# A fused feed-forward and window-attention kernel: the later chunks are normalised on GpSimd and not on ScalarE

## The chip, the cores and the metric

The kernel runs on one core of a Trainium2 chip. The metric is the device time of one execution in microseconds (us), as a median of three runs. The engines are TensorE (PE in the profile), VectorE (DVE), ScalarE (ACT), GpSimd (POOL) and SyncE (SP), which here issues most of the DMAs.

## The reference, cut to what matters

The input x is 4 batches of 2048 tokens with 256 numbers each, in float32. It goes through an expert layer, an attention layer and the same expert layer again, each of them on a layer norm of x and added to x:

```python
x = x + 0.5 * ffn(layernorm(x))      # 8 experts, top 2, an expert over its capacity is dropped
x = x + attn(layernorm(x))           # 16 heads of 16, |distance| <= 128, token 0 global
x = x + 0.5 * ffn(layernorm(x))

def layernorm(x, eps=1e-05):
    m = mean(x, axis=-1); v = var(x, axis=-1)
    return (x - m) / sqrt(v + eps)
```

With the inputs of this case every expert is over its capacity, so that the expert layers add nothing; the kernel counts this on the chip and then skips them. What is left is the attention over 4 x 2048 tokens and the counting. The layer norm ahead of the attention is what the change touches.

## The kernel before, in words

**Tiling.** A batch is 2048 tokens: 16 tiles of 128 tokens on the 128 partitions, or 4 chunks of 4 tiles. The 16 heads go in 4 groups of 4 heads. The main loop has 4 batches x 4 groups x 16 tiles = 256 steps of 4 quarters, one for each head of the group. In a quarter TensorE makes the scores of a query strip for the row maximum ("A", L1065), VectorE adds the mask and takes the maximum (L1514), TensorE makes the transposed scores of a tile 20 steps further back ("B", L1099), ScalarE takes their exponential (L1243), and TensorE multiplies probabilities with values ("PV", L1117), 23 steps back. At the end of each step GpSimd clears the two corners outside of the window in the exponentials of that B ("CUT", L1313 and L1318), once the fourth exponential is there; PV waits for it (`band_ready`).

**The layer norm of a chunk.** The input of the next batch is made ready while the loop runs on the batch before. SP loads a chunk into `x_ring`; VectorE takes the moments of its four tiles (L707, L709, "MOMENTS"); GpSimd makes `rstd`, `std_first` and `shift` of them (L720 to L734, "RSTD", the power at L728 first); then four instructions "NORM" write the tiles of `xn` (ScalarE at L1156, `scale * x + bias`), TensorE transposes them in two halves of two tiles ("XT", L890, p = 0 and p = 1) into two shared PSUM banks, and ScalarE copies each half out into `xnT` (L1175). The projections QK (L954) read that. ScalarE cuts their result into three bfloat16 pieces with VectorE and GpSimd (PIECE1 L1193, REST L1442, PIECE2 L1208, PIECE3 L1301), which SP stacks by DMA. In the first batch VectorE does the four NORMs of each chunk itself; so there are 3 x 4 = 12 chunks with 48 NORMs on ScalarE. They are the "later chunks" here.

**What sets the order.** Every engine walks the same list of events and runs its own in that order. The list is made by tables of quarters. Relative to the quarter at which a chunk begins, RSTD stands at 7, the NORMs at 12, 14, 16 and 18 and XT at 19. CUT stands at the end of a step. An engine runs in order, so that a waiting instruction holds all that is behind it on its engine.

The waits around the change: ScalarE's first NORM waits for `shift_ready` and for the transposes of the chunk before, of its second half (`xn` is one buffer). XT waits for `xn_ready`, 2 tiles for p = 0 and 4 for p = 1, and for its PSUM bank. The functions that the diff touches:

Of the kernel before, what the change touches and what calls it, by code (L numbers as in the profile page):

```python
# [7 lines left out]
ALU = mybir.AluOpType  # L8
# [41 lines left out]
def build(nc, x, wqk, wback, wv, wo, gate, w1, b1, w2, b2, consts, x1, out):  # L50
    ctx = ExitStack()
    with ctx:
        def sb(name, shape, dt=FP32):
# [10 lines left out]
        xn = sb("xn", [P, 4, D])  # L64
# [29 lines left out]
        mean_var = sb("mean_var", [P, 2, 4, 2])  # L94
# [41 lines left out]
                 "wqk_ready", "pads_ready", "k_ones", "v_pads", "wback_in",  # L136
                 "stats_ready", "moments_ready", "eps_added", "rstd_ready", "shift_ready", "xn_ready",
                 "base_ready", "logits_in", "move_ready", "moved", "fold_ready",
# [12 lines left out]
        S = sems  # L151
# [435 lines left out]
        def attend(nb, dram, batch_at, tiles_at, first):  # L587
# [123 lines left out]
            def deviations(pool, i):  # L711
# [6 lines left out]
                if i >= 2 and order[i - 2][0] == "EARLY":  # L718
                    pool.wait_ge(*normed(i - 2))
                pool.tensor_scalar(var_eps[:, :], mean_var[:, i % 2, :, 1], EPS, None, ALU.add)\  # L720
# [77 lines left out]
            def run_sync(sp):  # L798
# [17 lines left out]
                    for kind, *n in events:  # L816
                        if kind == "LOAD":
                            i, = n
                            if i in slot_of:
                                m, lap = slot_of[i]  # L820
                                if lap:
                                    before = ring[ring.index(i) - 3]
                                    if before in store_of:
                                        sp.wait_ge(S["moments_ready"], 4 * (before + 1))
                                        sp.wait_ge(*store_of[before])
                                    else:
                                        sp.wait_ge(*normed(before))
# [43 lines left out]
            def run_tensor(pe):  # L871
# [272 lines left out]
            def run_scalar(act):  # L1144
# [4 lines left out]
                    for kind, *n in events:  # L1149
                        if kind == "NORM" and not on_vector(n[0]):  # L1150
                            i, t = n
                            if t == 0:
                                act.wait_ge(S["shift_ready"], i + 1)
                                if early_count[i]:
                                    act.wait_ge(*filled("XT", early[early_count[i] - 1], 1))
                            act.activation(xn[:, t, :], x_tiles(i)[:, t, :], ACT.Identity,  # L1156
                                           bias=shift[:, i % 2, t:t + 1], scale=rstd[:, i % 2, t:t + 1])\
                               .then_inc(S["xn_ready"], 1)
                        elif kind == "FOLD_IN":
# [100 lines left out]
            def run_gpsimd(pool):  # L1260
                    for kind, *n in events:
                        if kind == "RSTD":
                            deviations(pool, *n)
                        elif kind == "FILL":
                            pool.memset(v_heads[:, :, 0:H, HD], 1.0).then_inc(S["v_pads"], 1)
# [73 lines left out]
            def run_vector(dve):  # L1339
# [12 lines left out]
                    for kind, *n in events:  # L1352
                        if kind == "MOMENTS":
                            moments(dve, *n)
                        elif kind == "NORM" and on_vector(n[0]):
                            i, t = n
                            if t == 0:
                                dve.wait_ge(S["rstd_ready"], i + 1)
                                if early_count[i]:
                                    dve.wait_ge(*filled("XT", early[early_count[i] - 1], 1))  # L1360
                            dve.tensor_scalar(xn[:, t, :], x_tiles(i)[:, t, :], mean_var[:, i % 2, t, 0:1],
                                              rstd[:, i % 2, t:t + 1], ALU.subtract, ALU.mult)\
                               .then_inc(S["xn_ready"], 1)
                        elif kind == "ROUTE":
# [186 lines left out]
                        elif kind == "OUT_MULT":  # L1551
                            n, = n
                            g, quartet = divmod(n, 4)
                            if g == 0:
                                dve.wait_ge(*normed(early_index[0, quartet]))
                            elif g % NG == 0:
                                dve.wait_ge(*filled("TURN_ATTN", late_index[g // NG - 1, quartet], 1))
# [131 lines left out]
```

## Time and profile before

| | us |
|---|---|
| median of 3 runs (852.82 to 858.6) | 853.02 |
| the profiled execution | 855.22 |
| its span in the profile | 853.5 |
| PE busy | 812.3 (95%) |
| DVE busy | 743.6 (87%) |
| ACT busy | 633.6 (74%) |
| POOL busy | 480.4 (56%) |
| the 48 NORMs on ACT (L1156) | 29.0 |

An engine's busy time is the union of its instructions' spans. "Idle before" is the time for which the engine stood still ahead of an instruction, with who ended it. The granted TensorE clock is at its full level in all 40 slices of the profile.

### The profile page before, as it was taken

Reading aid. Unit: us, or ns where it says so; the run is one execution under the profiler, and the core shown is the slowest. Engines: PE = TensorE matmul, PEld = TensorE weight load, DVE = VectorE, ACT = ScalarE, POOL = GpSimd, SP = SyncE. Lnnn points to the kernel's source line nnn. Section 1 sums busy time; section 2 is a strip of 40 time slices with the busy share of each in tenths; the row PEclk is TensorE's granted clock in tenths of the full one; section 3 lists DMA queues with packets and bytes.
Section 4 is the critical chain, followed back from the end, with each engine's and each line's share of the span. In section 5 each row is a group of like instructions: output and inputs, shape, how many; then the busy total and the mean of one; then the engine's idle time right before and its main releaser. Section 6 shows DMA issues by size and latency. Waiting matters only on the chain.

```text
span 853.5 us, 50532 instructions
## 1 busy us (share of the span) xinstructions
PE 812.3 (95%) x21504; PEld 613.5 (72%) x21505; DVE 743.6 (87%) x2788; ACT 633.6 (74%) x1418; POOL 480.4 (56%) x856
## 2 busy tenths in 40 slices
PE   9798999999999999999999999999999999998897
PEld 8555667677788777667778777766777877766675
DVE  7798799998987899998988889998988789999864
ACT  2258978997877666898777766799777766788871
POOL 3212556775554475766554556767555546656772
PEclk9999999999999999999999999999999999999999
DMA  7632224342213335342222235533221233423003
GB/s 227 107 94 64 67 77 125 102 130 61 82 57 103 104 107 164 113 124 82 71 77 65 91 114 149 166 102 92 68 80 57 94 113 101 141 76 128 7 27 106
DMA packets 93210, 83.55 MB, mean 98 GB/s; under 512 B 17584, under 2 KB 92208, under 8 KB 92976
## 3 DMA queue, kind: packets, MB, share of 16 engines
q1 hardware_dynamic: 91376, 78.91, 30.6%
q8 instruction: 172, 2.82, 1.5%
q10 hardware_dynamic: 1600, 1.31, 1.0%
q14 instruction: 62, 0.51, 0.2%
HBM read 20.66 MB, written 8.39 MB: 34 GB/s over the span
## 4 chain that ended last, share of the span: by engine, by line
PE 71%; DVE 13%; ACT 9%; issue 4%; POOL 1%; DMA 1%; SPq 1%; ACTq 0%; DVEq 0%; POOLq 0%
PE bank L1117 14%; PE bank L1065 12%; PE bank L1099 12%; PE bank L954 11%; PE bank L969 7%; DVE bank L1514 6%; PE bank L937 6%; ACT probs L1243 4%; PE bank L1139 3%; PE bank L923 2%; PE bank L875 2%; PE bank L890 1%; DVE row_max L1514 1%; ACT pieces L1193 1%; ACT xn L1156 1%
## 5 line engine op out<-in xcount | busy, mean ns | idle before, releaser
L1243 ACT ACTIVATE probs<-bank 128x384 f32<-128x384 f32 (+1 forms) x1024 | 459.5, 481 | 141.5 <-PE bank L1099 125.2
L1514 DVE CUSTOM_DVE_ANT_0 bank<-bank,con 128x288 f32<-128x288 f32 x1024 | 494.5, 519 | 55.7 <-PE bank L1065 47.5
L1065 PE MATMUL bank<-k_stack,q_stack 96*32 96x288 bf16 x4096 | 326.8, 288 | 8.7 <-DVE row_max L1514 4.8
L1099 PE MATMUL bank<-q_stack,k_stack 99*32 99x288 bf16 (+3 forms) x4096 | 320.1, 284 | 11.4 <-ACT probs L1243 7.7
L1117 PE MATMUL bank<-probs,v_sb 128*32 128x128 f32 x5888 | 307.1, 272 | 5.9 <-issue 4.2
L1313 POOL TENSOR_SCALAR_AFFINE_SELECT probs<-probs 128x512 f32<-128x512 f32 x240 | 154.7, 645 | 176.2 <-ACT probs L1243 175.6
L1117 PEld LDWEIGHTS bank<-probs,v_sb 128*32 128x32 f32 x5888 | 194.6, 110 | 38.8 <-issue 8.0
L1065 PEld LDWEIGHTS bank<-k_stack,q_stack 96*32 96x32 bf16 x4096 | 128.2, 95 | 69.6 <-DVE row_max L1514 19.9
L1099 PEld LDWEIGHTS bank<-q_stack,k_stack 99*32 99x32 bf16 x4096 | 125.5, 95 | 68.3 <-ACT probs L1243 43.8
L1318 POOL TENSOR_SCALAR_AFFINE_SELECT probs<-probs 128x512 f32<-128x512 f32 x240 | 153.0, 637 | 18.2 <-ACT probs L1243 18.2
L954 PE MATMUL bank<-xnT,wqk_sb 128*32 128x256 f32 x2048 | 159.7, 381 | 0.6 <-DVE neg_max L1536 0.5
L1514 DVE DVE_READ_ACCUMULATOR2_ANT row_max<- 128x1 f32 x1024 | 144.2, 141 | 0.0
L1301 POOL TENSOR_TENSOR pieces<-rest,pieces 128x512 bf16<-128x512 f32 x64 | 74.5, 1163 | 62.7 <-ACT pieces L1208 62.4
L969 PE MATMUL bank<-wv_sb,xnT 128*32 128x272 f32 x1024 | 84.3, 393 | 1.7 <-ACT v_sb L1215 1.1
L937 PE MATMUL bank<-wo_sb,attnT 128*32 128x264 f32 x1024 | 72.2, 386 | 0.4 <-DVE x_ring L1422 0.2
L954 PEld LDWEIGHTS bank<-xnT,wqk_sb 128*32 128x32 f32 x2048 | 65.0, 111 | 6.0 <-ACT v_sb L1215 1.2
L1193 ACT ACTIVATE pieces<-bank 128x512 bf16<-128x512 f32 x64 | 38.3, 598 | 21.5 <-PE bank L954 20.8
L1442 DVE TENSOR_TENSOR rest<-bank,pieces 128x512 f32<-128x512 f32 x64 | 44.1, 689 | 6.3 <-ACT pieces L1193 6.1
L1208 ACT ACTIVATE pieces<-rest 128x512 bf16<-128x512 f32 x64 | 40.6, 635 | 7.5 <-DVE rest L1442 7.4
L1139 PE MATMUL bank<-con,o_raw 128*32 128x68 f32 x2048 | 44.0, 223 | 1.9 <-ACT o_raw L1256 1.5
L1330 POOL TENSOR_TENSOR glob_term<-v_all,p 128x272 f32<-128x272 f32 x64 | 41.4, 647 | 2.2 <-DVE v_all L1483 1.8
L707 DVE BATCH_NORM_STATS2 stats<-x_ring 128x6 f32<-128x256 f32 x100 | 42.1, 421 | 0.0
(123 smaller groups left out, 714.4 us busy)
## 6 DMA issues: line engine op xcount, KB each, us to landing
q_stack<-pieces SPq DMA_DIRECT2D x384, 64.0 KB, 2.7
k_stack<-pieces SPq DMA_DIRECT2D x364, 64.0 KB, 2.7
x_ring<-in_x SPq DMA_DIRECT2D x28, 512.0 KB, 4.7
out_x<-x_ring SPq DMA_DIRECT2D x15, 512.0 KB, 4.3
attn<-in_x SPq DMA_DIRECT2D x4, 512.0 KB, 6.3
wback_sb<-in_wback SPq DMA_DIRECT2D x8, 256.0 KB, 5.6
k_stack<-pieces ACTq DMA_DIRECT2D x20, 64.0 KB, 3.6
q_stack<-neg_max SPq DMA_DIRECT2D x48, 16.0 KB, 2.2
```

What stands on the lines that cost most here:

```text
L937: last = pe.matmul(bank_of("PROJECT", i, t)[SP * s:SP * (s + 1), 0:D + E], attnT[:, t // 2, k, at:at + SP], wo_sb[:, k, :], start=(k == 0) ...
L954: last = pe.matmul(bank_of("QK", g, c)[SP * s:SP * (s + 1), 256 * half:256 * (half + 1)], wqk_sb[:, g % NG, k, SP * s:SP * (s + 1)], xnT[: ...
L969: last = pe.matmul(bank_of("VALUES", b, t)[SP * s:SP * (s + 1), 0:D + HD], xnT[:, k, at:at + SP], wv_sb[:, k, :], start=(k == 0), stop=(k ...
L1065: last = pe.matmul(a_ring[i % len(a_ring)][SP * s:SP * (s + 1), 0:WIN], q_stack[g % 2][0:KROWS, h, q:q + SP], k_stack[g % 2][0:KROWS, h, q ...
L1099: last = pe.matmul(score_bank(i)[SP * s:SP * (s + 1), start:final], k_stack[g % 2][0:SROWS, h, WINDOW + P * j + SP * s:WINDOW + P * j + SP ...
L1117: last = pe.matmul(o_bank[SP * h:SP * (h + 1), P * (i % 4):P * (i % 4 + 1)], v_sb[:, j, VW * head:VW * head + SP], probs[:, j % 4, h, P * ...
L1139: last = pe.matmul(bank_of("TURN", n)[SP * s:SP * (s + 1), HG * VW * i:HG * VW * (i + 1)], o_raw[:, at:at + SP], take, start=True, stop=True)
L1243: act.activation(probs[:, j % 4, h, c0:c1], score_bank(i)[:, c0:c1], ACT.Exp, scale=LOGIT_SCALE).then_inc(S["exp_ready"], 1)
L1301: pool.tensor_tensor(pieces[i % PIECES][:, 2, :], rest[:, :], pieces[i % PIECES][:, 1, :], ALU.subtract).then_inc(S["piece3_ready"], 1)
L1313: pool.affine_select(out=part, in_=part, compare_op=ALU.is_ge, fill=0.0, base=0, pattern=[[0, HG], [1, P]], channel_multiplier=-1).then_in ...
L1318: pool.affine_select(out=part, in_=part, compare_op=ALU.is_ge, fill=0.0, base=0, pattern=[[0, HG], [-1, P]], channel_multiplier=1).then_in ...
L1514: dve.tensor_tensor_reduce(out=a_ring[i % len(a_ring)][:, 0:WIN], in0=a_ring[i % len(a_ring)][:, 0:WIN], in1=mask, scale=1.0, scalar=con[: ...
```

## The change

All four NORMs of each later chunk move from ScalarE to GpSimd, at the same places of the list of events. They are written there as VectorE does them in the first batch, `(x - mean) * rstd` with two per-partition operands, and not as `scale * x + bias`; so they wait for `rstd_ready` and not for `shift_ready`. The semaphore `xn_ready` becomes two, `normed0` and `normed1`, one for each half of a chunk: XT of half p waits for its own, and the first NORM of each half waits for the transposes of the same half of the chunk before. The other users of `xn_ready` wait for both.

```diff
+        NORM_ENGINES = ("gpsimd", "gpsimd")
...
-            def normed(i):
-
-                return S["xn_ready"], 4 * early_count[i + 1]
-
-            def on_vector(i):
-
-                return first and order[i][1] == 0
+            def normed(i, half):
+
+                return S[f"normed{half}"], 2 * early_count[i + 1]
+
+            def norm_engine(i, t):
+
+                return "vector" if first and order[i][1] == 0 else NORM_ENGINES[t // 2]
...
-                            pe.wait_ge(S["xn_ready"], 4 * early_count[i] + 2 * p + 2)
+                            pe.wait_ge(*normed(i, p))
...
-                        if kind == "NORM" and not on_vector(n[0]):
+                        if kind == "NORM" and norm_engine(*n) == "scalar":
                             i, t = n
-                            if t == 0:
+                            if t % 2 == 0:
                                 act.wait_ge(S["shift_ready"], i + 1)
                                 if early_count[i]:
-                                    act.wait_ge(*filled("XT", early[early_count[i] - 1], 1))
+                                    act.wait_ge(*filled("XT", early[early_count[i] - 1], t // 2))
...
+                        elif kind == "NORM" and norm_engine(*n) == "gpsimd":
+                            i, t = n
+                            if t % 2 == 0:
+                                pool.wait_ge(S["rstd_ready"], i + 1)
+                                if early_count[i]:
+                                    pool.wait_ge(*filled("XT", early[early_count[i] - 1], t // 2))
+                            pool.tensor_scalar(xn[:, t, :], x_tiles(i)[:, t, :], mean_var[:, i % 2, t, 0:1],
+                                               rstd[:, i % 2, t:t + 1], ALU.subtract, ALU.mult)\
+                                .then_inc(S[f"normed{t // 2}"], 1)
```

GpSimd's queue is where the order matters. The line numbers differ by a few in the changed kernel: L720 to L734 of before are L722 to L736, L1301 is L1313, L1313 and L1318 are L1325 and L1330, and the new NORM is L1273. This is GpSimd in the third chunk (c = 2) of the second batch, before, from RSTD on:

```order
L728 TENSOR_TENSOR rstd<-var_eps,neg_half 128x4
L732 TENSOR_TENSOR std_first<-var_eps,rstd 128x4
L734 TENSOR_TENSOR shift<-neg_mean,rstd 128x4
L1313 AFFINE_SELECT probs<-probs 128x4x128
L1318 AFFINE_SELECT probs<-probs 128x4x128
L1313 AFFINE_SELECT probs<-probs 128x4x128
L1318 AFFINE_SELECT probs<-probs 128x4x128
L1301 TENSOR_TENSOR pieces<-rest,pieces 128x512
L1313 AFFINE_SELECT probs<-probs 128x4x128
L1318 AFFINE_SELECT probs<-probs 128x4x128
```

and the same place with the change:

```order
L730 TENSOR_TENSOR rstd<-var_eps,neg_half 128x4
L734 TENSOR_TENSOR std_first<-var_eps,rstd 128x4
L736 TENSOR_TENSOR shift<-neg_mean,rstd 128x4
L1325 AFFINE_SELECT probs<-probs 128x4x128
L1330 AFFINE_SELECT probs<-probs 128x4x128
L1273 TENSOR_SCALAR xn<-x_ring,mean_var,rstd 128x256
L1325 AFFINE_SELECT probs<-probs 128x4x128
L1330 AFFINE_SELECT probs<-probs 128x4x128
L1273 TENSOR_SCALAR xn<-x_ring,mean_var,rstd 128x256
L1313 TENSOR_TENSOR pieces<-rest,pieces 128x512
L1273 TENSOR_SCALAR xn<-x_ring,mean_var,rstd 128x256
L1325 AFFINE_SELECT probs<-probs 128x4x128
```

The fourth NORM follows behind the L1330 that comes next. So the one for which XT of p = 1 waits stands behind three CUTs and PIECE3. In the second chunk (c = 1) the queue is RSTD, two CUTs, two NORMs, PIECE3, L1325, two NORMs, L1330; in the fourth (c = 3) it is RSTD, CUT, NORM, PIECE3, NORM, CUT, two NORMs, CUT (its first eight entries behind RSTD, two NORMs in one row):

```order
L1325 AFFINE_SELECT probs<-probs 128x4x128
L1330 AFFINE_SELECT probs<-probs 128x4x128
L1273 TENSOR_SCALAR xn<-x_ring,mean_var,rstd 128x256
L1313 TENSOR_TENSOR pieces<-rest,pieces 128x512
L1273 TENSOR_SCALAR xn<-x_ring,mean_var,rstd 128x256
L1325 AFFINE_SELECT probs<-probs 128x4x128
L1330 AFFINE_SELECT probs<-probs 128x4x128
L1273 TENSOR_SCALAR xn<-x_ring,mean_var,rstd 128x256 x2
```

On ScalarE the four L1156 are gone, and the exponentials (L1243) between which they stood follow each other. The order of TensorE and VectorE is the same row by row.

## Rows read from the trace of the kernel before

**Rows 1.** The page: busy time of the engines, and the chain that ended last

```profile
PE 812.3 (95%) x21504; PEld 613.5 (72%) x21505; DVE 743.6 (87%) x2788; ACT 633.6 (74%) x1418; POOL 480.4 (56%) x856
...
PE 71%; DVE 13%; ACT 9%; issue 4%; POOL 1%; DMA 1%; SPq 1%; ACTq 0%; DVEq 0%; POOLq 0%
```

**Rows 2.** Stretches of time, second batch (last row: fourth), busy time of each engine

```profile
core 0: us, PE busy (x) PEld busy (x) DVE busy (x) ACT busy (x) POOL busy (x), PEclk, DMA share, GB/s
152.80:157.80 5.00, 4.89 (x117) 3.78 (x105) 4.51 (x20) 4.64 (x14) 3.63 (x8) 1.00 0.23 70
164.60:169.30 4.70, 4.36 (x117) 2.51 (x106) 4.63 (x19) 4.62 (x12) 3.90 (x7) 1.00 0.27 88
175.20:180.50 5.30, 4.33 (x133) 2.92 (x125) 4.54 (x17) 5.30 (x14) 4.23 (x8) 1.00 0.61 119
180.50:188.30 7.80, 7.80 (x228) 6.29 (x228) 7.36 (x31) 6.93 (x17) 5.34 (x11) 1.00 0.27 88
188.40:193.20 4.80, 4.01 (x169) 3.14 (x157) 4.76 (x22) 4.80 (x13) 3.55 (x5) 1.00 0.23 73
...
576.60:581.90 5.30, 4.28 (x133) 2.64 (x125) 4.54 (x17) 5.30 (x14) 4.23 (x7) 1.00 0.73 132
```

**Rows 3.** Groups by line: out<-in, shapes, count | busy us, mean ns | idle before

```profile
L1330 POOL TENSOR_TENSOR glob_term<-v_all,p 128x272 f32<-128x272 f32 x64 | 41.4, 647 | 2.2 <-DVE v_all L1483 1.8 <-DVE bank L1543 0.4
...
L725 POOL TENSOR_SCALAR neg_mean<-mean_var 128x4 f32<-128x4 f32 x16 | 3.6, 226 | 1.3
...
L1306 POOL MEMSET wback_sb<- 128x256 f32 x4 | 1.2, 312 | 1.7 <-PE bank L998 1.7
...
L1156 ACT ACTIVATE xn<-x_ring,shift,rstd 128x256 f32<-128x256 f32 x48 | 29.0, 604 | 0.6 <-POOL shift L734 0.6
```

**Rows 4.** Timeline of GpSimd, second chunk (c = 1): start, us, instruction, idle before

```profile
166.35 0.63 POOL L1318 TENSOR_SCALAR_AFFINE_SELECT probs<-probs 128x512 f32<-128x512 f32 x1
167.79 1.16 POOL L1301 TENSOR_TENSOR pieces<-rest,pieces 128x512 bf16<-128x512 f32 x1 [0.80 <-ACT pieces L1208]
168.90 0.65 POOL L1313 TENSOR_SCALAR_AFFINE_SELECT probs<-probs 128x512 f32<-128x512 f32 x1
170.12 0.63 POOL L1318 TENSOR_SCALAR_AFFINE_SELECT probs<-probs 128x512 f32<-128x512 f32 x1 [0.56 <-ACT probs L1243]
```

**Rows 5.** Timeline of GpSimd, third chunk (c = 2)

```profile
175.17 0.64 POOL L1313 TENSOR_SCALAR_AFFINE_SELECT probs<-probs 128x512 f32<-128x512 f32 x1
175.76 0.63 POOL L1318 TENSOR_SCALAR_AFFINE_SELECT probs<-probs 128x512 f32<-128x512 f32 x1
176.35 0.63 POOL L1313 TENSOR_SCALAR_AFFINE_SELECT probs<-probs 128x512 f32<-128x512 f32 x1
...
178.57 1.16 POOL L1301 TENSOR_TENSOR pieces<-rest,pieces 128x512 bf16<-128x512 f32 x1 [1.00 <-ACT pieces L1208]
```

**Rows 6.** Timeline of GpSimd, fourth chunk (c = 3)

```profile
188.91 0.63 POOL L1318 TENSOR_SCALAR_AFFINE_SELECT probs<-probs 128x512 f32<-128x512 f32 x1
...
191.81 0.63 POOL L1318 TENSOR_SCALAR_AFFINE_SELECT probs<-probs 128x512 f32<-128x512 f32 x1
193.71 0.63 POOL L1313 TENSOR_SCALAR_AFFINE_SELECT probs<-probs 128x512 f32<-128x512 f32 x1 [1.26 <-ACT probs L1243]
```

**Rows 7.** Timeline of GpSimd, first chunk (c = 0)

```profile
156.06 0.34 POOL L1290 TENSOR_TENSOR p_arg<-s0T,row_max 128x60 f32<-128x60 f32 x1 [1.28 <-DVE row_max L1501]
...
157.09 0.63 POOL L1318 TENSOR_SCALAR_AFFINE_SELECT probs<-probs 128x512 f32<-128x512 f32 x1
```

**Rows 8.** Timeline of TensorE at XT of the first and fourth chunk

```profile
157.79 0.66 PE L890 MATMUL bank<-con,xn 128*128 128x128 f32 x4
158.93 0.30 PE L890 MATMUL bank<-con,xn 128*128 128x128 f32 x1 [0.48 <-DVE neg_max L1536]
...
193.15 1.09 PE L890 MATMUL bank<-con,xn 128*128 128x128 f32 x8
```

**Rows 9.** The same of the second and third chunk, windows that end inside XT

```profile
169.29 0.98 PE L890 MATMUL bank<-con,xn 128*128 128x128 f32 x7
...
180.49 0.76 PE L890 MATMUL bank<-con,xn 128*128 128x128 f32 x5
```

More of the change, by code:

```diff
@@ L136, in build @@
                  "wqk_ready", "pads_ready", "k_ones", "v_pads", "wback_in",
-                 "stats_ready", "moments_ready", "eps_added", "rstd_ready", "shift_ready", "xn_ready",
+                 "stats_ready", "moments_ready", "eps_added", "rstd_ready", "shift_ready", "xn_ready", "normed0", "normed1",
                  "base_ready", "logits_in", "move_ready", "moved", "fold_ready",
@@ L718, in deviations @@
                 if i >= 2 and order[i - 2][0] == "EARLY":
-                    pool.wait_ge(*normed(i - 2))
+                    for half in range(2):
+                        pool.wait_ge(*normed(i - 2, half))
                 pool.tensor_scalar(var_eps[:, :], mean_var[:, i % 2, :, 1], EPS, None, ALU.add)\
@@ L826, in run_sync @@
                                     else:
-                                        sp.wait_ge(*normed(before))
+                                        for half in range(2):
+                                            sp.wait_ge(*normed(before, half))
                                 sp.dma_start(x_tiles(i), rows(dram, i)).then_inc(S[f"x_ring{m}"], 16)
@@ L1149, in run_scalar @@
                     for kind, *n in events:
-                        if kind == "NORM" and not on_vector(n[0]):
+                        if kind == "NORM" and norm_engine(*n) == "scalar":
                             i, t = n
-                            if t == 0:
+                            if t % 2 == 0:
                                 act.wait_ge(S["shift_ready"], i + 1)
                                 if early_count[i]:
-                                    act.wait_ge(*filled("XT", early[early_count[i] - 1], 1))
+                                    act.wait_ge(*filled("XT", early[early_count[i] - 1], t // 2))
                             act.activation(xn[:, t, :], x_tiles(i)[:, t, :], ACT.Identity,
                                            bias=shift[:, i % 2, t:t + 1], scale=rstd[:, i % 2, t:t + 1])\
-                               .then_inc(S["xn_ready"], 1)
+                               .then_inc(S[f"normed{t // 2}"], 1)
                         elif kind == "FOLD_IN":
@@ L1263, in run_gpsimd @@
                             deviations(pool, *n)
+                        elif kind == "NORM" and norm_engine(*n) == "gpsimd":
[6 more added lines that the diff above has]
+                                               rstd[:, i % 2, t:t + 1], ALU.subtract, ALU.mult)\
+                                .then_inc(S[f"normed{t // 2}"], 1)
                         elif kind == "FILL":
@@ L1354, in run_vector @@
                             moments(dve, *n)
-                        elif kind == "NORM" and on_vector(n[0]):
+                        elif kind == "NORM" and norm_engine(*n) == "vector":
                             i, t = n
-                            if t == 0:
+                            if t % 2 == 0:
                                 dve.wait_ge(S["rstd_ready"], i + 1)
                                 if early_count[i]:
-                                    dve.wait_ge(*filled("XT", early[early_count[i] - 1], 1))
+                                    dve.wait_ge(*filled("XT", early[early_count[i] - 1], t // 2))
                             dve.tensor_scalar(xn[:, t, :], x_tiles(i)[:, t, :], mean_var[:, i % 2, t, 0:1],
                                               rstd[:, i % 2, t:t + 1], ALU.subtract, ALU.mult)\
-                               .then_inc(S["xn_ready"], 1)
+                               .then_inc(S[f"normed{t // 2}"], 1)
                         elif kind == "ROUTE":
@@ L1554, in run_vector @@
                             if g == 0:
-                                dve.wait_ge(*normed(early_index[0, quartet]))
+                                for half in range(2):
+                                    dve.wait_ge(*normed(early_index[0, quartet], half))
                             elif g % NG == 0:
```

## The prediction

> **What bounds the kernel now.** The page comes first. TensorE is busy for 95% of the span and holds 71% of the chain that ended last, VectorE 13% and ScalarE 9%; GpSimd is busy for 56% and holds 1% of it [rows 1]. By these averages ScalarE's work is mostly hidden and GpSimd has room. But the change touches only twelve short places, so the stretches decide. I cut the second batch at the four places where ScalarE normalises a chunk, from its first NORM to XT [rows 2]. In the third chunk (175.2 to 180.5) ScalarE is busy for all of 5.30 us and TensorE for 4.33; in the fourth 4.80 of 4.80 against 4.01; in the second 4.62 of 4.70 against 4.36, with VectorE at 4.63; in the first 4.64 of 5.00 against 4.89. The reader is to see two things. These are the places where ScalarE holds TensorE back, by 0.11, 0.34, 0.97 and 0.79 us: 2.2 us in a batch, 6.6 us in three. And between them, as from 180.5 to 188.3, TensorE is busy throughout, so that what XT loses or gains goes straight into the time. The last row of the group is the same chunk two batches later: 4.28 of 5.30 against 4.33 of 5.30. The batches repeat, and I work out one and multiply by three.
>
> The timelines of GpSimd come next [rows 4 to 7], because GpSimd's spare time is not spread evenly either: in the third chunk it is busy for 4.23 of 5.30 us ahead of XT [rows 2], and its queue there begins late, with the moments and RSTD. Last the start of XT on TensorE [rows 8, 9], which is what the new NORMs must be in time for.
>
> **What is removed.** 48 NORMs of 0.604 us on ScalarE, 29.0 us busy [rows 3]. Behind them stand the exponentials that free TensorE's score banks, so TensorE can reach XT earlier, at most by the idle time above: 6.6 us in all. ScalarE's 0.6 us of waiting for `shift` goes too; it lies within those stretches.
>
> **What is added: the price of a NORM on GpSimd.** No row has it: 128x256, one tensor in, two operations, two per-partition operands. The nearest rows: TENSOR_SCALAR over 4 elements takes 0.226 us (L725) [rows 3]; the one-input select over 512 takes 0.63 to 0.65 and the next one starts 0.59 after it [rows 4, 5]. A straight line between them gives 0.226 + 0.41 x 252/508 = 0.43 for 256 elements. I take 0.45 with a start-to-start distance of 0.40, since two per-partition operands are more than one constant. Below, the bound is a fill of 128x256, 0.31 (distance 0.26); above, a two-input operation over 272, 0.65 (distance 0.60) [rows 3]; the far bound is the two-input subtraction over 512, 1.16 (distance 1.11) [rows 4].
>
> The Trainium skill, GPSIMD Engine Reference, section "Engine selection", speaks against the change: elementwise work belongs to VectorE, as a two-input operation is about twice as slow on GpSimd, while a one-input one runs at about line rate. Its section "Elementwise — side-by-side cycle accounting" gives about 2.6 cycles an element for two inputs at 1.2 GHz. An estimate from that page for 256 elements is 555 ns if the per-partition operands counted like a second input, and the sum below would then be about +6 us in place of +2.6; with its 1.03 cycles for a short body it is 220 ns and a fixed part.
>
> **Where the NORMs land.** Each of the four chunks is followed through GpSimd's new queue, from a CUT that stands ahead of the NORMs and so stays where it is. A CUT costs 2 x 0.59, PIECE3 1.11 to the next start [rows 4].
>
> - Second chunk. The last CUT starts at 166.35, so GpSimd is free at 166.94. Two NORMs to 167.74; this lies in the 0.80 us for which it waited for PIECE2 anyway, and PIECE3 stays at 167.79. The next select starts at 168.90 and is done with its place at 169.49 [rows 4]. The last two NORMs end at 169.49 + 0.80 + 0.05 = 170.34. XT began at 169.29 [rows 9]; its eight transposes took 1.09 in all in the fourth chunk [rows 8], so p = 1 began near 169.84. Now it begins near 170.40: **+0.56**.
> - Third chunk. GpSimd is free at 176.35 [rows 5]. NORM to 176.75, CUT to 177.93, NORM to 178.33, PIECE3 to 179.44 (it waited for ScalarE until 178.57, with ScalarE's PIECE2 now earlier), NORM to 179.84, CUT to 181.02, NORM done at 181.47. XT of p = 1 began near 180.49 + 0.55 = 181.04 [rows 9], now near 181.52: **+0.5**.
> - Fourth chunk. Free at 188.91 + 0.59 = 189.50 [rows 6]. NORM, PIECE3, NORM to 191.41, CUT to 192.59, two NORMs done at 193.44. p = 1 began near 193.15 + 0.55 = 193.70 [rows 8], now near 193.50, if TensorE comes 0.2 earlier, and its 0.79 us of idle time allow for that: **-0.2**.
> - First chunk. The first two NORMs fall into the 1.28 us ahead of L1290 [rows 7]. The other two start at 157.09 + 0.59 = 157.68 and end at 158.53. p = 1 waits for its PSUM bank from VectorE (L1536) and begins at 158.93 [rows 8]: **0**. VectorE is the cover here; without it this chunk would gain at most its 0.11.
>
> Sum: 0.86 us a batch, **+2.6 us** in three. The point is that the 6.6 us TensorE could gain do not come through: it reaches XT earlier in the second and third chunk and then waits there for the last NORM. What is late next is `normed1`.
>
> **What costs nothing.** The selects behind the NORMs start up to 0.8 us later. In the fourth chunk the next one waited 1.26 us for exponentials [rows 6], so it has room; the L1318 behind the second chunk's NORMs goes from 170.12 to about 170.3 [rows 4]. The RSTDs and the CUTs right behind them stand ahead of the NORMs. SP's load of the next chunk waits for `normed` some half a microsecond longer and is issued far ahead of its use; no DMA is added. The finer semaphores take one wait away that had long been met. If this cover were gone, PV would wait for CUT, by the same 0.4 to 0.8 us a chunk, up to 7 us.
>
> The profiled execution took 855.22 us and its span is 853.5; the median is 853.02. The sum on the profiled execution gives 857.8. The prediction is for the median: 853.0 + 2.6 = **855.6 us**.
>
> **The rivals.**
>
> A. *The relief wins.* A NORM costs 0.31 like the fill. Then the second chunk comes to +0.27, the third to -0.1, the fourth to -0.76: -0.6 a batch, -1.8 in all, **851.2**. The limit, if GpSimd were never late, is 853.0 - 6.6 = 846.4. For it: the select's slope is that of a streaming operation. Against it: VectorE is busy for 4.76 of 4.80 in the fourth chunk [rows 2], so that TensorE can hardly come 0.76 earlier, and two operations are not a fill. Chance 0.22.
>
> B. *GpSimd becomes the bound: slower.* Place: `normed1`, for which XT of p = 1 waits. Price: 0.65 a NORM (distance 0.60). The second chunk becomes 166.94 + 1.20, PIECE3 to 169.25, select to 169.84, NORMs done at 171.09: +1.3. The third gains four times 0.20 on its 0.47: +1.3, the fourth +0.6, the first +0.05. That is 3.25 a batch, +9.8, **862.8**. By the same steps the sum turns from gain to loss at a NORM of 0.36, and passes 8.5 us at one of 0.62; that is the point from which this rival decides. For it: the operation has three things to read. [...] Chance 0.2.
>
> C. *The software path is slow*, 1.16 like the subtraction of L1301. Then +3.35, +3.3, +2.6 and +1.05 in the four chunks, 10.3 a batch, +31, **884**. Against it: that row has twice the elements and two inputs. Chance 0.05.
>
> That the NORMs do not move at all is excluded: the new order has them in GpSimd's queue.
>
> The forecast has 0.53. About 1% (8.5 us) is what a measurement of this kernel can tell from no change. Faster by more than that, under 844.5, lies below even the limit: 0.02. Slower by more, over 861.5, is the upper half of B and all of C: 0.17. Within: 0.81. The range goes from 850, which holds most of A, to 863, the end of B.
>
> **What would show it.** L1273 on GpSimd, 48 times, 0.40 to 0.50 us. No L1156. TensorE waits at XT (L893) for `xn` from GpSimd in the second and third chunk, 0.5 us and more each, where before it had exponentials to wait for. ScalarE's busy time falls by 29 us to about 605, GpSimd's grows by some 21 to about 502. PE's idle time moves from the exponentials to XT. Wrong would be: a NORM above 0.62 or below 0.35; PV waiting for CUT in more places than before; or VectorE's instructions getting longer while GpSimd normalises.

## The result, and the profile after

The changed kernel takes **913.6 us** (median of 4 runs, 912.2 to 915.9) against 852.9: a ratio of 1.0709, 95% interval 1.0675 to 1.0743. It is 61 us slower, where +2.6 was forecast and 863 was the end of the range. The profiled execution took 913.2 us, its span is 911.5.

The page of the changed kernel, busy time and the chain that ended last, and of section 2 the granted clock in 40 slices:

```profile
PE 836.1 (92%) x21504; PEld 623.3 (68%) x21505; DVE 747.1 (82%) x2788; ACT 620.4 (68%) x1370; POOL 537.8 (59%) x904
...
PEclk9999999789999999888999999997899999999999
...
PE 60%; POOL 14%; DVE 11%; issue 6%; ACT 4%; SPq 2%; DMA 2%; ACTq 0%; POOLq 0%; DVEq 0%
```

GpSimd went from 1% of the chain [rows 1] to 14%, while its busy share hardly moved, from 56% to 59%. The clock line, all nines before, has three dips, at the three groups of later chunks. The group of the new NORM, and the waits of TensorE at XT (who waited for whom: us in total, times, the longest):

```profile
L1273 POOL TENSOR_SCALAR xn<-x_ring,mean_var,rstd 128x256 f32<-128x256 f32 x48 | 58.5, 1223 | 0.0
```

```profile
PEld bank L893 <- POOL xn L1273: 45.0, 18, 4.3
PE bank L893 <- POOL xn L1273: 40.7, 14, 4.1
```

A NORM takes 1.223 us, twice the 0.604 of ScalarE [rows 3] and 2.7 times the 0.45 that the sum took. All 48 lie between 1.215 and 1.241, which speaks against contention, as that would make some longer than others. GpSimd's queue in the third chunk of the second batch, which answers to [rows 5]:

```profile
182.00 0.64 POOL L1325 TENSOR_SCALAR_AFFINE_SELECT probs<-probs 128x512 f32<-128x512 f32 x1
182.60 0.63 POOL L1330 TENSOR_SCALAR_AFFINE_SELECT probs<-probs 128x512 f32<-128x512 f32 x1
183.23 1.23 POOL L1273 TENSOR_SCALAR xn<-x_ring,mean_var,rstd 128x256 f32<-128x256 f32 x1
184.42 0.63 POOL L1325 TENSOR_SCALAR_AFFINE_SELECT probs<-probs 128x512 f32<-128x512 f32 x1
185.01 0.63 POOL L1330 TENSOR_SCALAR_AFFINE_SELECT probs<-probs 128x512 f32<-128x512 f32 x1
185.63 1.22 POOL L1273 TENSOR_SCALAR xn<-x_ring,mean_var,rstd 128x256 f32<-128x256 f32 x1
186.82 1.16 POOL L1313 TENSOR_TENSOR pieces<-rest,pieces 128x512 bf16<-128x512 f32 x1
187.96 1.23 POOL L1273 TENSOR_SCALAR xn<-x_ring,mean_var,rstd 128x256 f32<-128x256 f32 x1
189.14 0.65 POOL L1325 TENSOR_SCALAR_AFFINE_SELECT probs<-probs 128x512 f32<-128x512 f32 x1
189.74 0.64 POOL L1330 TENSOR_SCALAR_AFFINE_SELECT probs<-probs 128x512 f32<-128x512 f32 x1
190.36 1.23 POOL L1273 TENSOR_SCALAR xn<-x_ring,mean_var,rstd 128x256 f32<-128x256 f32 x1
```

GpSimd has no gap from 182.00 to 191.59. TensorE at the same place:

```profile
186.91 0.66 PE L893 MATMUL bank<-con,xn 128*128 128x128 f32 x4 [0.17 <-POOL xn L1273]
191.64 1.11 PE L893 MATMUL bank<-con,xn 128*128 128x128 f32 x4 [4.08 <-POOL xn L1273]
192.68 0.43 PE L1068 MATMUL bank<-k_stack,q_stack 96*32 96x288 bf16 x4
192.90 0.45 PE L1102 MATMUL bank<-q_stack,k_stack 99*32 99x288 bf16 x4
193.14 0.46 PE L1068 MATMUL bank<-k_stack,q_stack 96*32 96x288 bf16 x4
```

The second half of XT starts 0.05 us after the fourth NORM. And what follows is slower: four matmuls of L1068 or of L1102 took 0.30 us ahead of XT and take 0.43 to 0.46 behind it. Stretches of time around this wait; PEclk, the granted clock, is the third number from the end:

```profile
core 0: us, PE busy (x) PEld busy (x) DVE busy (x) ACT busy (x) POOL busy (x), PEclk, DMA share, GB/s
182.00:187.00 5.00, 4.69 (x149) 3.16 (x142) 4.78 (x18) 4.91 (x12) 5.00 (x8) 1.00 0.02 3
187.00:191.60 4.60, 0.56 (x4) 0.32 (x4) 1.52 (x7) 0.88 (x2) 4.58 (x5) 0.84 0.00 0
191.60:195.60 4.00, 3.96 (x52) 2.62 (x56) 1.72 (x7) 1.58 (x3) 1.63 (x3) 0.50 0.11 35
195.60:203.40 7.80, 7.56 (x245) 5.92 (x240) 6.80 (x26) 6.23 (x14) 5.07 (x11) 0.92 0.27 90
```

TensorE was idle for 4 us; during the wait its granted clock fell to the lower of its two levels (0.50, 1.2 GHz in place of 2.4), and it stayed there for 4 us of work. The same happens at all twelve waits for the fourth NORM (2.7 to 4.1 us): in the 3.5 us behind XT the granted clock is 0.50 to 0.55.

The trace of the kernel before has one such case, too short to show in the tenths of its 40 slices. Near the start TensorE waited 2.25 us for a DMA, and its clock was low afterwards:

```profile
26.82 0.43 PE L1065 MATMUL bank<-k_stack,q_stack 96*32 96x288 bf16 x8 [2.25 <-DMA q_stack<-pieces]
```

```profile
26.80:30.30 3.50, 3.48 (x42) 1.88 (x46) 1.69 (x8) 0.00 (x0) 0.00 (x0) 0.59 1.00 121
```

So there are two suspects, one beside the other: the length of the NORM in the queue ahead of XT, and the clock. The rivals: the split semaphores and the new waits; the place in the queue, whatever a NORM costs; ScalarE's relief, which should have paid something back.

### The profile page after: what moved, and what is told of

The parts are those of the page before. It is cut to its first block, busy times and chain, and to the rows that moved or that the text cites. A ratio compares the mean times of both kernels' runs of the same rounds, so it can differ in the third digit from the quotient of the medians.

```text
span 911.5 us, 50575 instructions
## 1 busy us (share of the span) xinstructions
PE 836.1 (92%) x21504; PEld 623.3 (68%) x21505; DVE 747.1 (82%) x2788; ACT 620.4 (68%) x1370; POOL 537.8 (59%) x904
## 4 chain that ended last, share of the span: by engine, by line
PE 60%; POOL 14%; DVE 11%; issue 6%; ACT 4%; SPq 2%; DMA 2%; ACTq 0%; POOLq 0%; DVEq 0%
PE bank L1120 12%; PE bank L1068 10%; PE bank L1102 9%; PE bank L957 9%; PE bank L972 6%; POOL xn L1273 6%; PE bank L940 6%; DVE bank L1526 5%; PE bank L1142 2%; POOL probs L1330 2%; POOL probs L1325 2%; ACT probs L1246 2%; PE bank L926 2%; POOL rstd L730 2%; DVE stats L708 1%
## 5 line engine op out<-in xcount | busy, mean ns | idle before, releaser
L1068 PE MATMUL bank<-k_stack,q_stack 96*32 96x288 bf16 x4096 | 331.4, 295 | 11.1 <-DVE row_max L1526 7.8
L1102 PE MATMUL bank<-q_stack,k_stack 99*32 99x288 bf16 (+4 forms) x4096 | 325.3, 291 | 6.3 <-ACT probs L1246 3.2
L1120 PE MATMUL bank<-probs,v_sb 128*32 128x128 f32 x5888 | 312.3, 279 | 2.6 <-issue 0.9
L1325 POOL TENSOR_SCALAR_AFFINE_SELECT probs<-probs 128x512 f32<-128x512 f32 x240 | 154.7, 645 | 181.6 <-ACT probs L1246 181.3
L1068 PEld LDWEIGHTS bank<-k_stack,q_stack 96*32 96x32 bf16 x4096 | 128.8, 98 | 79.6 <-DVE row_max L1526 25.4
L1102 PEld LDWEIGHTS bank<-q_stack,k_stack 99*32 99x32 bf16 x4096 | 127.2, 97 | 63.2 <-ACT probs L1246 39.1
L957 PE MATMUL bank<-xnT,wqk_sb 128*32 128x256 f32 x2048 | 164.9, 395 | 0.6 <-DVE neg_max L1548 0.5
L1330 POOL TENSOR_SCALAR_AFFINE_SELECT probs<-probs 128x512 f32<-128x512 f32 x240 | 153.0, 638 | 15.4 <-ACT probs L1246 15.4
L1313 POOL TENSOR_TENSOR pieces<-rest,pieces 128x512 bf16<-128x512 f32 x64 | 74.4, 1162 | 54.7 <-ACT pieces L1211 54.7
L893 PE MATMUL bank<-con,xn 128*128 128x128 f32 x128 | 24.0, 318 | 40.9 <-POOL xn L1273 40.7
L1273 POOL TENSOR_SCALAR xn<-x_ring,mean_var,rstd 128x256 f32<-128x256 f32 x48 | 58.5, 1223 | 0.0
L1178 ACT ACTIVATE xnT<-bank 128x512 f32<-128x512 f32 x32 | 18.8, 595 | 57.8 <-PE bank L893 57.5
L893 PEld LDWEIGHTS bank<-con,xn 128*128 128x128 f32 x128 | 15.6, 157 | 47.1 <-POOL xn L1273 45.0
```

The costliest lines, as they stand in the source:

```text
L957: last = pe.matmul(bank_of("QK", g, c)[SP * s:SP * (s + 1), 256 * half:256 * (half + 1)], wqk_sb[:, g % NG, k, SP * s:SP * (s + 1)], xnT[: ...
L1068: last = pe.matmul(a_ring[i % len(a_ring)][SP * s:SP * (s + 1), 0:WIN], q_stack[g % 2][0:KROWS, h, q:q + SP], k_stack[g % 2][0:KROWS, h, q ...
L1102: last = pe.matmul(score_bank(i)[SP * s:SP * (s + 1), start:final], k_stack[g % 2][0:SROWS, h, WINDOW + P * j + SP * s:WINDOW + P * j + SP ...
L1120: last = pe.matmul(o_bank[SP * h:SP * (h + 1), P * (i % 4):P * (i % 4 + 1)], v_sb[:, j, VW * head:VW * head + SP], probs[:, j % 4, h, P * ...
L1273: pool.tensor_scalar(xn[:, t, :], x_tiles(i)[:, t, :], mean_var[:, i % 2, t, 0:1], rstd[:, i % 2, t:t + 1], ALU.subtract, ALU.mult)\
L1313: pool.tensor_tensor(pieces[i % PIECES][:, 2, :], rest[:, :], pieces[i % PIECES][:, 1, :], ALU.subtract).then_inc(S["piece3_ready"], 1)
```

## The experiments

Medians are for the kernel and for the kernel before on the same chip; the ratio has its 95% interval. It is taken from all runs and can differ a little from the ratio of the two medians.

**The semaphores alone.**

```diff
-        NORM_ENGINES = ("gpsimd", "gpsimd")
+        NORM_ENGINES = ("scalar", "scalar")
```

> All four NORMs are back on ScalarE, with the two new semaphores and the waits of the change kept. Theory (the loss is the length of GpSimd's NORM, 1.22 us, on the way to XT): the semaphores cost nothing, within 2 us of the kernel before (853), ScalarE's L1156 form again 48 x 0.60. Rival (the split of the semaphores or the new waits hold something up): it stays well above 853, up to 913.

Measured: 853.0 against 853.2, ratio 0.9998 (0.9971 to 1.0026), L1159 on ScalarE x48 at 0.605 us. The semaphores and the new waits cost nothing that can be measured, within 0.3%.

**NORMs over 64 and over 20 columns.** The same kernel as the change, with

```diff
-                            pool.tensor_scalar(xn[:, t, :], x_tiles(i)[:, t, :], ...
+                            pool.tensor_scalar(xn[:, t, 0:64], x_tiles(i)[:, t, 0:64], ...
```

> The change with each NORM over 64 columns in place of 256 (the other columns of xn are left as they are, so three quarters of the layer norm of batches two to four are left out); same queue, same order, same waits. Theory (length alone): if the price is per element, 1.22 us falls to about 0.45 us, which is the price that the prediction took, and the time must come out at its sum, 855.6, between 850 and 860. Rival (place in the queue: the fourth NORM stands behind three CUTs and PIECE3 whatever it costs): the waits at XT stay, over 2 us a chunk, and the time stays above 880. If the price is per instruction and not per element, the NORM stays above 1.0 us and the time above 900.

Measured: 867.3 against 853.2, ratio 1.0147 (1.0096 to 1.0198). The NORM took 0.588 and not 0.45, and TensorE's waits at XT were 13.6 us in place of 40.7. Neither figure of the expectation came; the price is part fixed, part per element. By the walk through the queue, a NORM of 0.588 is worth about +8 us, and the time rose by 13. Part of the rest is the clock. TensorE waited 1.83, 2.14 and 2.34 us at XT of the third chunk in the second, third and fourth batch. Its clock was low behind the first two, and there the end of the next XT slipped by 2.3 and 2.2 us against the kernel before, where it slipped by 0.65 in the batch whose clock stayed up:

```profile
183.60:187.10 3.50, 3.50 (x64) 2.56 (x63) 2.33 (x9) 1.96 (x4) 1.84 (x3) 0.53 0.20 66
388.90:392.40 3.50, 3.50 (x65) 2.38 (x68) 2.15 (x9) 1.75 (x4) 1.84 (x3) 0.55 0.16 56
595.30:598.80 3.50, 3.50 (x104) 2.87 (x108) 3.15 (x13) 2.89 (x7) 1.84 (x3) 1.00 0.19 61
```

A second size, with 20 columns in place of 64:

> The change with each NORM over 20 columns (the rest of the layer norm of batches two to four is left out). From the 256 and the 64 columns measured, 1.22 and 0.587 us, the price should be 0.375 + 20 x 0.0033 = 0.44 us, which is the 0.45 that the prediction took. Theory (only the size of the price was wrong): the prediction's sum must then hold, about 2.6 us over the kernel before, between -1 and +6. Rival (the hand walk through GpSimd's queue was wrong as well, as 64 columns gave +14 where the same steps give about +8): +9 or more.

```profile
L1273 POOL TENSOR_SCALAR xn<-x_ring,mean_var,rstd 128x64 f32<-128x64 f32 x48 | 27.9, 588 | 0.0
```

```profile
L1273 POOL TENSOR_SCALAR xn<-x_ring,mean_var,rstd 128x20 f32<-128x20 f32 x48 | 20.7, 435 | 0.0
```

Measured: 858.2 against 853.4, ratio 1.0073 (1.0041 to 1.0106), that is +6.2 us (3.5 to 9.0) with a NORM of 0.435, close to the price that the prediction took. The sum said +2.6, which lies outside of this interval; the theory's "-1 to +6" and the rival's "+9 or more" both touch it, so the time alone does not decide between them. Chunk by chunk in the second batch, the end of XT slipped further against the kernel before by 0.75, 0.7 and 0.0 us in the second, third and fourth chunk; the prediction had +0.56, +0.5 and -0.2. The walk is thus some 0.2 us a chunk short, some 2 us in all. The profile has another piece elsewhere: behind a stall of 1.36 us at L1142 ahead of the fourth batch the clock was 0.52 for 3.5 us.

**What makes the instruction dear.** Four forms of it, one for each tile of a chunk:

```diff
+                            mean, dev = mean_var[:, i % 2, t, 0:1], rstd[:, i % 2, t:t + 1]
+                            tile = x_tiles(i)[:, t, :]
+                            if t == 0:
+                                done = pool.tensor_scalar(xn[:, t, :], tile, 0.5, 2.0, ALU.subtract, ALU.mult)
+                            elif t == 1:
+                                done = pool.tensor_scalar(xn[:, t, :], tile, mean, None, ALU.subtract)
+                            elif t == 2:
+                                done = pool.tensor_tensor(xn[:, t, :], tile, mean.to_broadcast([P, D]), ALU.subtract)
+                            else:
+                                done = pool.tensor_scalar(xn[:, t, :], tile, 0.5, None, ALU.subtract)
...
```

> A price list: in each later chunk the first tile gets subtract and multiply with two constants, the second a subtract with one per-partition operand, the third a two-input subtract with the mean broadcast, the fourth a subtract with one constant, all 128x256 on GpSimd (so the layer norm of batches two to four is left out). If the per-partition operands make the NORM dear, the two with constants alone take 0.4 to 0.5 us and the one with one per-partition operand stands between them and 1.22. If the number of operations does, the first is near 1.22 and the fourth near 0.45. If every TENSOR_SCALAR of this width costs 1.2, all of these do and the two-input one (about 0.62 by L1330 of before) is the cheapest.

The instructions of `xn` in this kernel: duration in ns as least, median, most:

```profile
L1276 POOL TENSOR_SCALAR xn<-x_ring x12: 1086/1087/1103, 151.8 to 621.0; 128x256 f32<-128x256 f32 x12
L1278 POOL TENSOR_SCALAR xn<-x_ring,mean_var x12: 931/937/942, 152.9 to 623.2; 128x256 f32<-128x256 f32 x12
L1280 POOL TENSOR_TENSOR xn<-x_ring,mean_var x12: 612/616/624, 155.5 to 625.3; 128x256 f32<-128x256 f32 x12
L1282 POOL TENSOR_SCALAR xn<-x_ring x12: 848/854/861, 156.0 to 625.8; 128x256 f32<-128x256 f32 x12
```

One constant costs 0.854, a second constant and operation 0.23 more; one per-partition operand costs 0.937, two cost 1.223. The two-input TENSOR_TENSOR of the same size takes 0.616. So the per-partition operands are not the main part of what makes the NORM dear (0.08 to 0.14 of 1.22 us): each of the four TENSOR_SCALARs measured at this width is dearer than the two-input operation, and 0.65, which the prediction had as the upper end, is below the cheapest of them. (The time of this kernel, 1650.5 us in one run, says nothing about the change: its trace has the matmuls of the expert layer, L306, which the kernel before does not run. It seems that without this layer norm some experts are under their capacity.)

**The clock.**

```diff
-                            pe.wait_ge(*normed(i, p))
                             claim(pe, "XT", i, p)
+                            if p == 1 and order[i][1] > 0:
+                                for _ in range((11, 13, 16, 11)[order[i][2]]):
+                                    pe.matmul(bank_of("XT", i, p)[:, 0:P], ones[:, :], ones[:, :], start=True, stop=True)
+                            pe.wait_ge(*normed(i, p))
```

> The change with 11, 13, 16 and 11 matmuls of ones (two instructions each, 0.12 us an instruction in the warm-up of the kernel) ahead of TensorE's wait for the second half of each later chunk, written to the bank that the transposes then overwrite: they fill the wait of 3 to 4 us with work. Theory (two costs: the wait itself, and TensorE at half clock for 3.4 to 6.8 us from each wait on): the clock stays at 1.0, the waits remain as busy time, and the time falls by 10 to 20 us, to 893 to 903. Rival (only the wait itself counts): it stays at 911 to 916.

Measured: 894.0 against 853.2, ratio 1.0465 (1.0414 to 1.0516): 19.6 us less than the change, by work that computes nothing. In the same chunk of this kernel:

```profile
183.81 0.38 PE L896 MATMUL bank<-con,xn 128*128 128x128 f32 x2
184.02 3.74 PE L892 MATMUL bank<-ones 128*128 128x128 f32 x32
188.20 0.55 PE L896 MATMUL bank<-con,xn 128*128 128x128 f32 x3 [0.44 <-POOL xn L1276]
```

```profile
184.00:188.30 4.30, 3.86 (x35) 3.67 (x34) 0.48 (x3) 0.60 (x1) 4.15 (x5) 1.00 0.00 0
188.30:192.30 4.00, 4.00 (x108) 3.21 (x112) 3.08 (x13) 2.85 (x6) 1.84 (x3) 1.00 0.18 56
```

The clock stays at 1.00 through the wait, and in the 4.0 us behind it TensorE does 108 matmuls where it did 52 at half clock. So about a third of the loss was the clock, and the expectation's 893 to 903 was met.

**Half of the NORMs, early or late in the queue.** `NORM_ENGINES = ("gpsimd", "scalar")`:

> The change's code with GpSimd for the first two tiles of each later chunk and ScalarE for the last two. By GpSimd's queue with 1.20 us from start to start the two are done at 157.2, 169.3, 179.9 and 193.0 on the time scale of the kernel before, where XT of p = 0 began at 157.79, 169.29, 180.49 and 193.15: in time, just. ScalarE is relieved of 14.5 us. Theory (a NORM on GpSimd costs only where XT waits for it): no wait at XT above 0.5 us, the time is 849 to 856, so the same or a little faster than before. Rival (the longer GpSimd queue delays PIECE3 and CUT, and these hold TensorE): waits of PV for GpSimd and 860 or more.

Measured: 854.4 against 853.4, ratio 0.9998 (0.9983 to 1.0014), as the theory had it. TensorE's waits at XT for GpSimd are 1.6 us, none over 0.4, with 24 NORMs of 1.229. The mirror, `("scalar", "gpsimd")`:

> ScalarE for the first two tiles of each later chunk and GpSimd for the last two, the mirror of the run with GpSimd first. By GpSimd's queue with 1.20 us from start to start the fourth NORM now ends at 160.1, 171.9, 183.3 and 194.8 on the time scale of the kernel before, 1.2, 2.1, 2.3 and 1.1 us after XT of p = 1 began: 6.7 us a batch, 20 us in all. Theory (only what stands late in the queue costs): 868 to 880. Rival (half of the NORMs costs half of the loss wherever they stand): near 883 here, and the other half would have cost as much, which it did not; or nothing at all, 853.

Measured: 884.1 against 853.8, ratio 1.0324 (1.0267 to 1.0381), with 23.9 us of waits at XT against the 20 expected, and a mean granted clock of 0.984. The same number of NORMs on GpSimd costs nothing in one place and 28 us (30 by the medians) in the other. The time is above the 868 to 880 and at the rival's "near 883"; but the other half cost nothing, so that this rival, half of the NORMs for half of the loss, is wrong. What the expectation left out is the clock, and here its part can be told apart from that of the wait. The second chunk waited 2.35 us at XT in each of the three batches, and these are the 3.5 us behind XT:

```profile
173.40:176.90 3.50, 3.50 (x61) 2.35 (x64) 1.93 (x7) 1.58 (x3) 0.04 (x1) 0.50 0.54 101
385.20:388.70 3.50, 3.50 (x109) 2.92 (x112) 3.13 (x13) 2.64 (x6) 1.04 (x4) 1.00 0.94 201
593.40:596.90 3.50, 3.50 (x57) 2.36 (x60) 1.91 (x7) 1.58 (x3) 0.07 (x1) 0.50 1.08 235
```

In the third batch, whose clock stayed at 1.00 behind all four waits, the end of XT slipped by 0.9, 2.3, 2.5 and 1.4 us in the four chunks, 7.1 in all, against the 6.7 of the walk; in the second and fourth batch by 14.1 and 11.5. Why waits of the same length lower the clock in one batch and not in another stays open.

**The NORMs right behind RSTD.**

```diff
+        LATER = {'LOAD': -20, 'MOMENTS': (1, 3, 5, 7), 'RSTD': 7, 'NORM': (8, 9, 10, 11), 'XT': 19}
...
-                        opening(at + EARLY["NORM"][t], "NORM", i, t)
+                        opening(at + plan["NORM"][t], "NORM", i, t)
```

> The change with the NORMs of the later chunks at quarters 8, 9, 10 and 11, right behind RSTD, in place of 12, 14, 16 and 18; loads, moments, RSTD and XT stay. By GpSimd's queue the fourth NORM then ends 0.2 to 0.7 us after XT of p = 1 began on the time scale of the kernel before, so XT hardly waits. But the corners (CUT) that stood ahead of the NORMs come 1.2 to 4.8 us later, and the PV that needs them has 0 to 2 us of room: about 2.6, 3.9, 1.2 and 1.9 us in the four chunks, 9.6 a batch. Theory (GpSimd's 4.9 us a chunk have no free place; the wait only changes its name): waits of PV for L1331 of some 20 to 30 us, 870 to 890. Rival (the order of the queue was the fault): 853 to 860.

Measured: 897.3 against 853.8, ratio 1.0506 (1.0452 to 1.0559). The waits:

```profile
PEld bank L1121 <- POOL probs L1331: 35.8, 20, 3.8
...
PE bank L1121 <- POOL probs L1331: 29.8, 15, 3.5
```

XT no longer waits for GpSimd; PV waits for the corners in its place, 29.8 us. The waits are the 29 expected. The time is over the 890, and the clock was low here too: 0.973 in the mean, and 0.50 for 3.5 us behind PV's wait of 3.2 us in the second batch. The wait only changed its name: this part of GpSimd's queue has no free 4.9 us.

**All of it a step and a half earlier**, and its control with ScalarE:

```diff
+        LATER = {'LOAD': -24, 'MOMENTS': (-5, -3, -1, 1), 'RSTD': 1, 'NORM': (6, 8, 10, 12), 'XT': 19}
```

> The change with loads, moments, RSTD and NORMs of the later chunks six quarters (about 4 us) earlier in the list of events, XT where it was (load four quarters earlier). The 48 NORMs on GpSimd still take 1.22 us. Theory (lateness at XT is all that hurts, directly and through the clock): the waits of 2.9 to 4.1 us at XT all but vanish, the clock stays full, and the time comes to 846 to 858, the lower end if ScalarE's relief is worth the 6.6 us of the prediction. Rival (GpSimd has no room for 58 us in these stretches, so its corners come late for PV): waits for L1325 and L1330 take the place of those for xn, and it stays above 870.

> The control of the run before: the same earlier places, but all four NORMs on ScalarE. Theory: as nothing waited for the moments on TensorE's path before, moving them earlier is worth nothing by itself, 851 to 856. Rival (the earlier places alone are worth something, and the run before owes its time to them): under 850.

Measured: GpSimd early 873.6, ratio 1.0226 (1.0210 to 1.0243); ScalarE early 870.9, ratio 1.0187 (1.0172 to 1.0203). The first expectation's 846 to 858 was missed; its rival's "above 870" was met, but not for the rival's reason, as the control shows. Both expectations of the control were wrong: the earlier places cost some 16 us by themselves, whoever normalises. In the control's trace TensorE waits longer for VectorE's maxima (10.6 us at L1069 against 4.6 in the run with the semaphores alone) and for exponentials (11.0 against 7.9); no run shows more of why. Against that control, GpSimd's 48 NORMs of 1.222 us cost about 3 us more than ScalarE's and not 61, and no wait at XT for GpSimd is left. The 3 us are a net figure: PV waits 6.5 us for L1331 and TensorE 6 us more for VectorE's maxima (L1069 and L1079), while its waits for exponentials fall from 11.0 to 3.1.

**What ScalarE's relief is worth.** NORMs over 20 columns on ScalarE, which took 9.7 of its 29.0 us away:

> ScalarE keeps all the NORMs of the later chunks, as before, but each over 20 columns only (the rest of the layer norm of batches two to four is left out); GpSimd does none. This is ScalarE's relief by itself, about 48 x 0.35 = 17 us of its time, with nothing added anywhere. Theory of the prediction (ScalarE holds TensorE back by 6.6 us there): 846 to 850, 3 to 6 us under the kernel before. Rival (the relief is worth nothing, because VectorE and the corners from GpSimd hold TensorE at the same places): within 1.5 us of the kernel before.

Measured: 851.1 against 853.8, ratio 0.9974 (0.9950 to 0.9998). The expectation's 17 us of relief were wrong, 0.403 us are left of a NORM; the 2.2 us gained would fit a full worth of 6.6 as well as a ceiling. So the whole relief, with almost nothing put on GpSimd:

```diff
-                            pool.tensor_scalar(xn[:, t, :], x_tiles(i)[:, t, :], mean_var[:, i % 2, t, 0:1],
-                                               rstd[:, i % 2, t:t + 1], ALU.subtract, ALU.mult)\
-                                .then_inc(S[f"normed{t // 2}"], 1)
+                            pool.memset(xn[:, t, 0:4], 0.0).then_inc(S[f"normed{t // 2}"], 1)
```

> The change with each NORM on GpSimd replaced by a fill of 4 columns, about 0.10 us by L1294 of before (so batches two to four are not normalised at all). The run with 20 columns on ScalarE took only 9.7 of its 29 us away and gained 2.2 us, so the worth of the whole relief is still open. Here ScalarE is free of all 29 us and GpSimd's queue is almost as before. Theory of the prediction (TensorE gains what ScalarE held it back by): up to 6.6 us under the kernel before, 846 to 849. Rival (relief past the first microseconds is worth nothing, since VectorE holds TensorE next, as the run with half of the NORMs on GpSimd, 14.5 us of relief for no gain, suggests): 1 to 3 us under the kernel before.

Measured: 851.7 against 854.3, ratio 0.9962 (0.9940 to 0.9984): 3.2 us (1.4 to 5.1), half of the 6.6. By the medians it is 2.6. Both expectations touch this interval; it excludes the 6.6. TensorE's waits, before and in this run (L1099 is L1102 here, L1065 is L1068):

```profile
PE bank L1099 <- ACT probs L1243: 7.7, 21, 1.3
PE bank L1065 <- DVE row_max L1514: 4.8, 15, 0.8
```

```profile
PE bank L1102 <- ACT probs L1246: 3.3, 8, 1.3
PE bank L1068 <- DVE row_max L1524: 6.8, 21, 0.8
```

It waits 4.4 us less for ScalarE's exponentials and 2.0 us more for VectorE's maxima: by these waits nearly half of the relief is lost to VectorE.

None of the versions that compute the layer norm beats the kernel before beyond its interval. By the last run the relief of ScalarE is worth at most some 5 us as long as the rest of the list of events stays as it is.

## Why the prediction was wrong, point by point

**What bounds the kernel and where: right.** XT in the twelve chunks was the place; `normed1` came late, in the chunks named, and the loss on TensorE went straight into the time.

**The price of a NORM: the step that failed.** "I take 0.45 with a start-to-start distance of 0.40": it is 1.22 with 1.20. The straight line ran from a TENSOR_SCALAR of 4 elements to a *select* of 512 [rows 3 to 5], and took for granted that a longer TENSOR_SCALAR moves its elements at the select's pace. By the three sizes measured this one costs about 0.37 us and 3.3 ns an element; the line had 0.81 ns. The bound above, 0.65, rested on two inputs as the worst case. The trace disagrees with the Trainium skill here, GPSIMD Engine Reference, section "Engine selection", by which a one-input operation is near line rate and two inputs are the slow case: at 256 columns the two-input subtract took 0.616 us and the one-input one with one constant 0.854. The measurement decides. The advice of the Trainium skill not to give GpSimd such work held, but not by the rule that it gives.

Only rival C had a price of this size, 1.16, from the one row that looked least alike, at a chance of 0.05. Its argument against, "twice the elements and two inputs", was the same guess again. Its time, 884, was still 30 us short; 20 of these are the clock, of which it had no term either. A kind of instruction that no row shows at its size has no upper bound from its cousins.

**The walk through GpSimd's queue: right in place and nearly in size.** With a distance of 1.20 the same steps give +2.3 (two NORMs of 2.4 us no longer fit the 1.28 us of idle time, [rows 7]), +3.7, +3.6 and +2.9 us, 12.5 a batch, 37.5 in all. With the clock held up, the end of XT moved in the second, third and fourth chunk of the second batch by 3.7, 3.9 and 3.2, and by 3.1 in the first of the third, and the time by 41 us. In the changed kernel itself it moved by 5.5, 5.7, 5.2 and 4.2: the rest is the clock. At the price that the prediction took, though, the walk's 0.2 us a chunk too little are as large as most of its sum: the run with 20 columns came to +6.2 and not to +2.6. A NORM of that price would have brought the time inside the range of 850 to 863, and still above the forecast.

**The clock: not in the sum at all.** No term asked what an idle TensorE of 3 to 4 us does to its own clock. It cost 19.6 us here, on top of the 41 of the waits. The trace of the kernel before had the case in it, a clock of 0.59 behind a wait of 2.25 us, and the kernel gave a hint: its warm-up and first batch carry matmuls of ones that compute nothing.

**The relief of ScalarE: half of the size.** The 6.6 us were TensorE's idle time in four stretches [rows 2]; 3.2 came through. VectorE was busy for 4.63 of 4.70 and 4.76 of 4.80 us in two of them. The prediction had noted both, but brought them up only against rival A's gain in the fourth chunk and not against the 6.6; with ScalarE relieved, TensorE's waits for VectorE grew by 2.0 us.

**What costs nothing.** PIECE3, CUT, the loads and the semaphores cost nothing while XT was the late one: PV's waits for corners in the changed kernel are 2.3 and 1.1 us in all (L1325, L1330), against 1.4 and 2.3 before. "If this cover were gone, PV would wait for CUT" is what the run with the NORMs behind RSTD shows, with 29.8 us in place of "up to 7", by the price again.

The sum on what was measured: waits with a full clock, relief counted in, +41; clock +20; together the 61.

## What to carry to other kernels

An engine that is busy for 56% can still be without a gap for 10 us in front of the one thing that the critical engine waits for: walk its queue from the last fixed point to the wait, with each instruction's start-to-start distance, before giving it more. If the trace does not hold the instruction at its size and in its form, run it once before the sum is worth anything, and until then let the far rows carry a real chance. For a wait that lands on TensorE, look up in the trace at hand what its clock did behind waits of that length, and allow for it: here the clock fell behind all twelve waits of 2.7 to 4.1 us, and behind some of those of 1.8 to 2.6 us. When such a wait can't be avoided, fill it: matmuls in its place gave back a third of the loss here.

## What the runs showed of the hardware

- GpSimd, 128 partitions, float32, 256 columns: subtract with one constant 0.854 us, with one per-partition operand 0.937; subtract and multiply with two constants 1.087, with two per-partition operands 1.223 (0.588 at 64 columns, 0.435 at 20); two-input subtract with a broadcast operand 0.616. The select over 512 takes 0.64 [rows 4].
- ScalarE's scale-and-bias takes 0.605 us over 256 columns and 0.403 over 20: some two thirds of it do not depend on the size.
- TensorE's granted clock went from 1.00 to 0.50 during waits of 2.7 to 4.1 us at XT and stayed there for microseconds of full work, in twelve cases of twelve; with matmuls in the same place it stayed at 1.00. Behind waits of 1.8 to 2.6 us at XT it was low in seven cases of twelve (64 columns, and GpSimd for the last two tiles), with waits of 2.35 us on both sides.
